# The normalised rows of the mix: not stored, but made again from x by ScalarE in the row stage; softmax chain 32 steps ahead instead of 36, stock of onehots six instead of eight

## What is computed

```python
xn = layernorm(x)
# the graph part
h_s, z = xn @ W_self.T, xn @ W_func.T
e = leaky_relu(concat(z[src], z[dst], edge_attr) @ W_att.T)
alpha = softmax of e over the edges of one target
agg = segment_sum(alpha * z[src], dst)
gnn = xn + relu(h_s + agg where a node has edges, else xn)
# the mix
q, k, v = xn @ Wq + bq, xn @ Wk + bk, xn @ Wv + bv        # 8 heads, phi(q), phi(k)
out = phi(q) (phi(k)^T v) / (phi(q) sum(phi(k)))
m = layernorm(xn + out @ Wo + bo)
mix = layernorm(m + relu(m @ W1 + b1) @ W2 + b2)
x = x + gnn + mix
# the experts
y = layernorm(x)
p = softmax(relu(y @ router_w1 + b) @ router_w2 + b)
x = x + sum over the two best experts of weight * three-layer expert(y)
```

## Time and profile before

| | before |
|---|---|
| time, median of 3 runs | 2011.67 us (2006.14 to 2014.0) |
| time of the profiled execution | 2011.9 us |
| its span | 2010.1 us |
| busy share of the span: PE, DVE, ACT, POOL | 87%, 68%, 56%, 66% |
| node stage and keys, 0 to 182 us: PE, DVE, ACT, POOL busy | 144, 120, 86, 91 us |
| step loop, 182 to 1478 us | 1151, 916, 784, 997 us |
| row stage up to the routing, 1478 to 1549 us | 54, 49, 30, 0 us |
| routing, 1549 to 1565 us | 8, 13, 3, 0 us |
| rest of the row stage, 1565 to 1626.5 us | 44, 42, 31, 43 us |
| expert stage, 1626.5 to 2010 us | 343, 222, 192, 199 us |

### The profile page before, as it was taken

One profiled execution on the slowest core, in us unless ns is written; L12 is line 12 of the kernel. 1 busy time (PEld: TensorE's weight loads), 2 busy tenths in 40 slices (PEclk: granted clock), 3 DMA queues, 4 the chain that ended last, 5 costly groups with the idle time before them and its releaser, 6 DMA issues.

```text
span 2010.1 us, 37149 instructions
## 1 busy us (share of the span) xinstructions
PE 1743.8 (87%) x9369; PEld 1376.5 (68%) x9369; DVE 1362.5 (68%) x3962; ACT 1126.3 (56%) x3395; POOL 1329.7 (66%) x1106
## 2 busy tenths in 40 slices
PE   6789888988898899889989899889876789989994
PEld 5556556766676677667667667667545679978994
DVE  6766665767677777677867777666666846446566
ACT  4446654666565666565656565566644445545562
POOL 5078786888878878888888888777400615677631
PEclk9989997999999999899999999899888989999997
DMA  8979964776777777668776676665369625645466
GB/s 243 266 181 213 201 159 111 160 172 167 171 177 174 170 169 172 158 165 197 166 168 166 169 179 159 154 150 140 92 162 210 177 77 145 169 125 149 142 180 198
DMA packets 311614, 336.93 MB, mean 168 GB/s; under 512 B 132623, under 2 KB 259803, under 8 KB 311406
## 3 DMA queue, kind: packets, MB, share of 16 engines
q1 hardware_dynamic: 171862, 187.74, 36.9%
q0 software_dynamic: 130720, 138.83, 29.4%
q10 hardware_dynamic: 8823, 7.99, 1.3%
HBM read 253.32 MB, written 79.99 MB: 166 GB/s over the span
## 4 chain that ended last, share of the span: by engine, by line
PE 56%; DMA 13%; DVE 12%; issue 7%; POOL 5%; SPq 2%; ACT 2%; DVEq 2%; ACTq 0%; POOLq 0%
PE bank L831 54%; DMA wexp<-func_rows,a_src 7%; DVE acc L1981 4%; POOL wexp L767 3%; POOL sorted_d L779 2%; DMA g_all<-sorted_d 2%; DMA work<-mix_rows 1%; DVEq L1981 1%; PE bank L1167 1%; SPq L471 1%; DMA attr_s<-in_attr 1%; SPq L467 1%; PE bank L998 1%; DVE attr_s L1617 1%; DVE work L1817 1%
## 5 line engine op out<-in xcount | busy, mean ns | idle before, releaser
L767 POOL DMA_INDIRECT wexp<-func_rows,a_src x850 | 1061.3, 1249 | 330.9 <-issue 194.9
L1981 DVE SCALAR_TENSOR_TENSOR acc<-acc,corr,bank 125x257 f32 x850 | 403.6, 475 | 287.2 <-PE bank L831 233.3
L831 PE MATMUL bank<-wexp,onehot 125*125 125x257 f32 x1700 | 567.9, 431 | 21.1 <-DVE acc L1981 17.2
L1351 ACT ACTIVATE onehot<-iota_r,a_rel 125x125 f32<-125x125 f32 x850 | 334.7, 394 | 238.2 <-PE bank L831 235.9
L831 PEld LDWEIGHTS bank<-wexp,onehot 125*125 125x125 f32 x1700 | 312.6, 203 | 100.2 <-ACT onehot L1359 30.4
L1359 ACT ACTIVATE onehot<-onehot,a_p 125x125 f32<-125x125 f32 x850 | 329.6, 388 | 0.0
L779 POOL DMA_INDIRECT sorted_d<-acc,work x100 | 121.7, 1217 | 223.0 <-ACT acc L1421 131.7
L831 PE MATMUL bank<-g_all,wexp 128*128 128x128 f32 x1840 | 231.5, 280 | 8.2 <-issue 7.3
L831 PEld LDWEIGHTS bank<-g_all,wexp 128*128 128x128 f32 x1840 | 220.8, 196 | 10.2 <-issue 9.1
L831 PE MATMUL bank<-work,w_s 128*128 128x250 f32 x800 | 215.2, 392 | 0.0
L831 PE MATMUL bank<-w_s,work 128*125 128x256 f32 x800 | 210.5, 385 | 4.5 <-ACT work L1342 3.4
(11 more groups left out here) (304 smaller groups left out, 2526.5 us busy)
## 6 DMA issues: line engine op xcount, KB each, us to landing
rel_oh<-rel_d SPq DMA_DIRECT2D x50, 531.2 KB
attr_s<-in_attr SPq DMA_DIRECT2D x100, 224.0 KB
sorted_d<-spare SPq DMA_DIRECT2D x72, 257.0 KB
work<-in_x SPq DMA_DIRECT2D x71, 224.0 KB
g_all<-sorted_d SPq DMA_DIRECT2D x115, 128.5 KB
work<-xnT_d SPq DMA_DIRECT2D x59, 250.0 KB
wexp<-func_rows,a_src POOLq DMA_INDIRECT x850
g_all<-y_d SPq DMA_DIRECT2D x32, 224.0 KB
```

Source lines behind the costliest of these rows:

```text
L767: pool.indirect_dma_start(ring[:, n % RING, :], None, func_rows, bass.IndirectOffsetOnAxis(ap=a_src[:, n // CS, n % CS:n % CS + 1], axis=0 ...
L831: return pe.matmul(o, l, r, start=first, stop=last_, **kw)
L1351: act.activation(onehot[:, n % AHEAD, :], iota_r[:], ACT.Abs, bias=a_rel_v[:, n:n + 1], scale=-1.0).then_inc(s("far"), 1)
L1981: v.scalar_tensor_tensor(to, to, corr[:, k % 2, y:y + 1], bank[stepping[n % 3]][0:R, 0:D + 1], ALU.mult, ALU.add).then_inc(s("summed"), 1)
```

## The change

`xn_rows`, `xn_out` and `m_normal` go. `x_again(g)` now waits for the residual of group g-1 (`m_xx`) and for a mark of the mix (`m_z`) in place of the store. In the row stage `group_in` loads x where it loaded `xn_rows`, and the new `row_xn(g)` of ScalarE normalises the two blocks in place, behind `row_rstd(g-1)`; `rows(g)` on DVE waits for it. The loops keep their 36 positions of lead-in, but the softmax chain is counted from `SOFT` = 32 steps ahead: every step of the tables comes four positions later, `k_u` at 17k-24 and `a_p` at 17k-7, and so do the loads of a run's columns. `STOCK` is 6, so ScalarE first uses `a_p` at 17k-6.

```diff
-LEAD = 36
+LEAD, SOFT = 36, 32
...
-STOCK = 8
+STOCK = 6
...
-        xn_rows = nc.dram_tensor("xn_rows", (N, D), F32).ap()
...
-            return [(k, n + LEAD - RUN * k) for k in range(max(0, (n + LEAD) // RUN - 1), min(RUNS, (n + LEAD) // RUN + 1))]
+            return [(k, n + SOFT - RUN * k) for k in range(max(0, (n + SOFT) // RUN - 1), min(RUNS, (n + SOFT) // RUN + 1)) if n + SOFT >= RUN * k]
...
-                freed(sp, s("xn_out"), 32 * (g - 1))
+                freed(sp, s("m_xx"), 2 * (g - 1))
+                freed(sp, s("m_z"), 2 * g)
                 load_rows("m_x_in", m_xs[g % 2], rows_of(x, g))
-
-            def xn_out(g):
-                sp.wait_ge(s("xn_made"), 2 * (GROUPS - HELD + g + 1))
-                load_rows("xn_out", rows_of(xn_rows, g), m_xs[g % 2])
...
-                    if n == RUN * k - 47:
+                    if n == RUN * k - 43:
                         relative_in(k)
-                    if n == RUN * k - 41:
+                    if n == RUN * k - 37:
                         run_in(k)
...
-                    if at == 43:
-                        xn_out(g)
...
-                for to, rows in ((c_xn, xn_rows), (c_x2, mix_rows)):
+                for to, rows in ((c_xn, x), (c_x2, mix_rows)):
                     load_rows(f"group_in{g % CBUF}", to[g % CBUF], rows_of(rows, g))
...
-            sp.wait_ge(s("xn_out"), 32 * GROUPS)
...
-            def m_normal(g):
-                act.wait_ge(s("m_xx"), 2 * (g + 1))
-                for j in range(2):
-                    b = 2 * g + j
-                    act.activation(m_xs[g % 2][:, j], m_xs[g % 2][:, j], ACT.Identity, bias=nmr[:, b:b + 1],
-                                   scale=rstd_all[:, b:b + 1]).then_inc(s("xn_made"), 1)
-
...
-                    if at == PERIOD + 11:
-                        m_normal(g)
...
+            def row_xn(g):
+                act.wait_ge(s(f"group_in{g % CBUF}"), 32 * GIN[g % CBUF] + 80 * (g // CBUF + 1))
+                for j in range(2):
+                    b = 2 * g + j
+                    act.activation(c_xn[g % CBUF][:, j], c_xn[g % CBUF][:, j], ACT.Identity, bias=nmr[:, b:b + 1],
+                                   scale=rstd_all[:, b:b + 1]).then_inc(s("xn_made"), 1)
...
                     row_rstd(i - 1)
+                if i < GROUPS:
+                    row_xn(i)
...
                 v.wait_ge(s(f"group_in{g % CBUF}"), 32 * GIN[g % CBUF] + 80 * (g // CBUF + 1))
+                v.wait_ge(s("xn_made"), 2 * (GROUPS - HELD + g + 1))
```

## The result

| | before | changed |
|---|---|---|
| median | 2010.92 us (12 runs, 2006.07 to 2018.44) | 2019.99 us (12 runs, 2009.84 to 2025.07) |
| ratio | | 1.0048, interval 1.0029 to 1.0066 |
| the profiled execution, its span | 2011.9, 2010.1 us | 2025.07, 2023.2 us |

The changed kernel is slower, by about 9.7 us, 6 to 13 by the interval. Two further comparisons on the chip gave 1.0032 (1.0011 to 1.0053) and 1.0036 (1.0007 to 1.0064), that is 6.4 and 7.2 us, so the cost is rather 7 or 8 us. Forecast were 1.6 us less. The time lies inside the range of 1999 to 2023, the sign is wrong. The profiled execution of the changed kernel, 2025.07 us, is the slowest of its twelve, 5 us above their median.

A forecast was written before the change was run, and what follows sets the result against it. The prediction took the step loop as bound by the gathers and the row stage by a DVE-ScalarE ping-pong. From 2011.9 us, ring waits -9, tail -4.5 and row stage +11.9 gave 2010.3 us, 8-in-10 range 1999 to 2023.

The forecast's parts named there:

- What bounds the loop: Step loop: bound by POOL's gathers at a cadence of 1.51 us, not PE; consumers have 1.6 us a run to spare.
- Rival (c): Step loop, run boundary: waiting for a_p costs consumers more than 1.6 us a run; at 2.1 us, 2043 us; chance 0.06.
- Ring waits: Step loop: POOL's waits for a free ring slot shrink with the later chain, 9 us saved, ends 3 and 11.5.
- Rival (a): Step loop: hardly gains, ring waits stay and only the tail is saved; 2019.3 us; chance 0.18.
- Tail: Step loop's end: 41 steps instead of 45 after the last gather, 4.5 us saved, ends 3.5 and 5.
- Period of the row stage: Row stage: row_xn behind Exp lengthens a group's period from 4.48 to 5.48 us; groups 14 to 24 cost +10.0.
- Groups 0 to 14: Row stage's first part: +3.4 us to group 13, mostly hidden by the loads' 5.6 us, and +1.0 for the routing.
- The end of the row stage: Last group to layer 1: POOL's sends are later than the rows, so 2.5 us of the added time come back.
- Rival (b): Row stage: PE falls to 1.2 GHz and bounds ten groups, 17 us more, so 2027 us; chance 0.08.
- Rival (d): Row stage: rows cost little, POOL's sends (+4.4) set the tiles' start; 1999.8 us; chance 0.21.

The follow-up runs named there:

- e6_soft30: Changed kernel with row_xn ahead of row_rstd on ScalarE, softmax chain 30 steps ahead and a stock of four: 1994.6 us, ratio 0.9932 to the kernel before.
- after_again: The changed kernel unaltered, run once more for a second profile; the two repeats of the changed kernel gave ratios 1.0032 and 1.0036.
- e2_rows: Kernel before with only the row stage's half (no xn_rows, ScalarE normalises x behind Exp), chain 36 ahead, stock eight: 2028.02 us, ratio 1.0084.
- e4_dve_head: Changed kernel with the normalisation on DVE at the head of rows(g), behind the wait for Exp, in place of row_xn: 2008.24 us, ratio 0.9999.
- e3_swap: Changed kernel with two calls exchanged, row_xn(i) ahead of row_rstd(i-1) on ScalarE: 2000.11 us, ratio 0.996 to the kernel before.

## Why the prediction was wrong, point by point

Means of the three profiles of each: first gather 103.1 and 107.1, to the last gather 1331.6 and 1323.9, to the last step 45.0 and 41.5, to the first tile 146.9 and 162.3, to the end 382.4 and 381.1. That is +4.0 - 7.7 - 3.5 + 15.4 - 1.3 = +6.9 us, in line with the timed 6.4, 7.2 and 9.7.

- **What bounds the loop: right.** The cadence of the gathers stayed, DVE's waits for them stayed, and PE's or ScalarE's own waits cost nothing: ScalarE waits 38 us for a_p in the changed kernel and 68 in e6_soft30, which is faster. Rival (c) is out.
- **Ring waits: right.** Forecast 9 us saved; 11.0 to 1.2 in the mean, 9.8, good to about 1 us. Long gathers took 2 us more (34.4 and 36.5), which their spread of 25.6 to 39.7 doesn't let anyone put down to the change. Rival (a) is out by the trace, although its 2019.3 is nearly the measured time: the loss sits in the row stage.
- **Tail: 3.5 instead of 4.5.** The term was priced by four steps right behind the wait, which have pieces of the chain and of the mix between them (4.87 us). Those pieces are still behind the wait (1440.17 to 1445.18 for the first four steps of the changed kernel, 5.01 us); what left it are four bare steps, at 0.85 us each as in the last two rows of DVE above.
- **Period of the row stage: right.** 5.48 forecast and measured, groups 14 to 24 took 54.8 us instead of 44.8, the routing 0.8 more. The profile names the cause as forecast, DVE waiting for ScalarE's new line.
- **Groups 0 to 14: mis-sized**, +4.4 forecast (3.4 and 1.0 for the routing), +6.3 measured. The step took the 5.6 us of the loads as a fixed pace that hides the longer period. It is a draw: from group 0 to 14 the kernel before took 85.8, 83.0 and 82.5 us, and the profile that the forecast rests on is the slowest; against that one alone the term is right, 90.1 - 85.8 = 4.3. The changed kernel took 90.1, 89.8 and 90.2, since DVE and ScalarE bound it there and no longer the loads.
- **The end of the row stage: the step that failed by its mechanism.** Forecast were 2.5 us back, because the rows had been waiting for POOL's sends. It came in one of three profiles. From group 24 to the first tile are 16.5 us before and 16.3, 14.2 and 16.3 now. The windows of that stretch, first the changed kernel's first profile, then the kernel before (granted clock in the third column from the right):

```profile
1623.30:1639.60 16.30, 12.90 (x46) 10.57 (x44) 4.96 (x18) 6.23 (x16) 1.78 (x2) 0.50 0.18 50
```

```profile
1610.00:1626.50 16.50, 10.14 (x47) 8.50 (x46) 5.53 (x20) 6.38 (x15) 7.95 (x7) 0.74 0.32 87
```

  PE is at 1.2 GHz for the whole of it, and the last groups' router is on the path, first the changed kernel, then before:

```profile
1633.56 2.00 PE L824 MATMUL bank<-work,rw_s 128*128 128x250 f32 x4 [0.35 <-DVE work L2105]
```

```profile
1619.35 1.08 PE L831 MATMUL bank<-work,rw_s 128*128 128x250 f32 x4 [0.35 <-DVE work L2111]
```

  So DVE's last logits come 13.8 us behind group 24 instead of 11.6, and the 2.2 us eat the room. In after_again, with a granted clock of 0.76 there, it was 14.2, close to the 14.0 of the forecast (16.5 - 2.5). The two variants that also have the pair behind Exp, e2_rows and e4_dve_head, bear it out: granted clock 0.50 and 16.3 us in both. Where the pair stands ahead of Exp the low clock costs nothing, 16.5 us at 0.50 in e3_swap, because the sends are the later ones there.
- **Rival (b), PE at the low clock**, was thus half there, at a place that the forecast hadn't priced. Over groups 14 to 24 the granted clock was 0.88 and not 1.00, but PE's work still fitted into 5.48 us. Between groups 14 and 23 the low level was never granted for as long as a period, so what ten groups at that level would take stays untested; it cost 2 us, where nothing else was left to hide it, and not 17. The Trainium skill (TensorE: Matmul & The Clock Gate, HAM oscillation) describes such work in pieces as falling to the low clock again and again; the rows agree with the falling, and its price was what stood exposed.
- **Rival (d)**, sends that set the start of the tiles: out. The last send starts at 1624.19 in the changed kernel, 15.5 us ahead of the first tile; before, the last one was 7.9 us ahead.
- **Node stage: no term at all.** The first gather behind it varies by 9.5 us between executions of like kernels. With a sum of terms as small as -1.6 us, the sign hung on terms that were known to 2 or 3 us each.

The loop's -11.2 against -13.5 and the row stage's +15.4 against +11.9 are 5.8 us of the 8.5 by which the means miss the forecast; the node stage's 4.0 less 1.3 at the end are the rest. Of the row stage's 3.5 us, 1.9 are groups 0 to 14 and 1.6 the end (0.9 us back in the mean instead of 2.5). The end is the step with the wrong mechanism: it took the room behind the sends as free and left out that DVE's last logits come later when PE's clock is low. It doesn't carry the sign alone. With the row stage as forecast the means would still give +3.4 us, and the node stage's 4.0, for which the forecast had no term and whose cause stays open, are more than that.

## What to carry to other kernels

When work is added to two engines that wait for each other, the side of the exchanged value on which it stands can matter more than its length or its engine: on ScalarE, behind Exp it cost 1.0 us a group, ahead of it 0.02. Look for the engine that waits before the exchange, and put it there. A pace set by transfers is a draw, not a floor to hide work under, and room at the end of a stage counts only if all that becomes late next, the clock too, has been priced.

## What the runs showed of the hardware

The ring waits of gathers 135, 136 and 140 came out the same in all three profiles of the kernel before and in e2_rows, 1.78, 2.83 and 1.87 us beyond the cadence, though the first gather started up to 2.1 us apart: that stretch is fixed by the program. Against that, the summed length of long gathers went from 25.6 to 39.7 us and the first gather from 101.3 to 110.8, without a pattern by kernel in the long gathers and without a settled one in the first gather. Four router matmuls of 128x250 took 1.08 us at the high clock and 2.00 at a granted clock of 0.50. In all 14 profiles the median gather took 1.211 to 1.214 us and the median idle time to the next was 0.304 or 0.305, wherever the chain stood.
